# GpSimd's constants at the head of its program, two scalings on ScalarE, first tokens in two transfers, other priorities in a macaron transformer layer

## The chip, the cores and the metric

The kernel runs on one core of one Trainium2 chip, in one launch. The metric is the device time of that core in microseconds (us); lower is better. The core's engines are TensorE (PE in the rows; its weight loads are PEld), VectorE (DVE), ScalarE (ACT), GpSimd (POOL) and the queue that issues the transfers, SyncE (SP).

## The reference, cut to what matters

Eight batches of 512 tokens of width 256 in float32 pass through a feed-forward block with an attention over the 16 heads of each single token and 8 experts, through an attention over the 512 tokens of a batch with 8 heads, and through the first block again with the same weights.

```python
x = hidden_states                                     # (8, 512, 256)
x = x + 0.5 * ffn(layernorm(x))
x = x + attn(layernorm(x))                            # 8 heads of 32, softmax over 512 keys
x = x + 0.5 * ffn(layernorm(x))

def ffn(x):
    h = rmsnorm(x, gamma1)
    q = h @ Wq + bq                                   # 16 heads of 16
    k, v = split((h @ Wdown + bdown) @ Wup + bup)     # 256 -> 64 -> 512
    att = softmax(q k^T / 4) over the 16 heads of the same token
    x = x + (att v) @ Wo + bo
    h2 = rmsnorm(x, gamma2)
    gate = softmax(h2 @ Wg + bg)                      # 8 experts
    return x + sum_e gate[e] * (h2 @ We[e])
```

## The kernel before

All tokens stay in SBUF in `X` (128 partitions, 8 batches, 4 tiles of 128 tokens, 256). Products are made of float32r pairs: an operand is held as a high and a low part (`_hi`, `_lo`) and three products are added. A feed-forward block of one batch is a **job**: jobs 0 to 7 are the first pass, 8 to 15 the second (`k` in the code; B is 8). Each job has these steps, and a step is one entry in an engine's program:

- `stats` (VectorE, L1020 and L1024: mean and variance of four tiles) and `norm` (GpSimd, L1530 to L1542: seven small instructions that make the factors; for job 0 it is cut into `norm_first`, L1504 to L1516, and `norm_outer`).
- `xs` (GpSimd, L1563): the tokens scaled, in two halves p of two tiles each. `hT` (TensorE, L757) transposes a half, `hT_hi` (ScalarE, L1315) and `hT_lo` (VectorE, L1074) take it out of PSUM.
- `down`, `q`, `key`, `val` (TensorE products, L503), `q_turn`, `key_turn`, `val_turn` (VectorE, L1100, L1111, L1124), `key_P`, `key_A`, `val_P`, `val_A` (GpSimd L1571 and ScalarE L1338: the copies that the products per token need), `scores` (TensorE, L673, 64 small products), `top`, `exp`, `at`, `attend` (TensorE, L683), and so on to the `expert` products (L503 with `we`), whose sums are added by VectorE (`add`, L1236) and by ScalarE and GpSimd (`y` L1390, `ysum` L1616 to L1621).
- Between the two passes the attention over tokens runs: `score` (TensorE L906), `max` (VectorE L1262), `shift` (TensorE L916), `a_exp` (ScalarE L1453), `a_total` (VectorE L1268), `normalise` (GpSimd L1665, 64 times), `values` (TensorE L932), `a_add` (GpSimd L1626). For job 8 `xs` also waits for the attention's last transposes out of the same buffer (`a_hT`), and fills the last column of its tokens with ones first (L1560, a memset).

GpSimd's program starts with constants (L1483 to L1493). Four more, the step `blank` (L1518 to L1522: `la_one`, the zero halves of `qc`, `one_v`, `at`), stand in its order after `norm_outer`. TensorE's program starts with 16 transposes of nothing (L712) and has 10 and 16 more ahead of key(0, 1) and scores(0).

The head also prepares weights: `last` and `columns`, `spread`, `fold`, `gate_fold`, `gate_last`, `gate_row` bring gamma and the biases into the weights; `gate_out` (TensorE, 12 products of 8 columns with `late`) and `gate_wo` (VectorE, L1058 to L1060) add the gate's columns to `wo`; `split_hi` (ScalarE L1276) and `split_lo` (VectorE L990) make the two parts; `we_lo` (GpSimd L1552) does it for the experts. `split_lo` 1, the low part of `wq`, must be there before q(0, 0).

What each engine does in which order is not written out. `all_steps` (L78) lists every step with its engine, a duration in ns and the steps it follows; `all_orders` (L298) plays them through: whenever an engine is free, it takes the step of highest rank among those that can start now. The rank is the longest way to the end of the program plus a weight for the kind of step (`SOONER`) and for the batch (`FIRST`); TensorE adds `SAME` for a step that uses the array the same way as the one before it (`ARRAY`: `score` in row tiles, `values`, `scores`, `attend` in column tiles). Durations and landing times in that list are the author's entries; the chip only runs the resulting orders, with semaphores between them. The order inside the attention over tokens is written out by hand (`ATTENTION`, L43), but which other step comes in between is chosen by rank. `stats` of jobs after 8 can only come after the attention's last `max`.

The transfers are issued by SP one after the other (L1681 on): the first batch's tokens in one transfer of 512 KB (L1678), then gamma's row, the last rows of two weights, the biases, the weights, the next batches.

Of the kernel before, what the change touches and what calls it, by code (L numbers as in the profile page):

```python
# [9 lines left out]
ACT = mybir.ActivationFunctionType  # L10
# [61 lines left out]

def parts_of(job, B):

    return 2 if job in (0, B) else 1


def all_steps(B, NT, KC):  # L78
# [8 lines left out]
    for s, landed in enumerate((4400, 12000, 16500, 18500)):  # L87
        put("SP", landed, ("tokens", s))
# [3 lines left out]
    for n, (landed, hi, lo) in enumerate(((5600, 300, 300), (7000, 650, 1300), (7700, 650, 0), (9500, 650, 1700),  # L92
                                          (12900, 650, 1300), (7600, 0, 0), (22500, 1900, 1250), (24500, 1900, 1250),
# [14 lines left out]
    put("PE", 640, ("spread", 0), ("last", 0))  # L108
    put("PE", 2560, ("spread", 1), ("last", 0))
# [3 lines left out]
    put("DVE", 250, ("gate_fold", 0), ("load", 5))  # L113
    put("PE", 400, ("gate_last", 0), ("gate_fold", 0))
    put("DVE", 250, ("gate_row", 0), ("gate_last", 0), ("load", 1))
    put("SP", 13300, ("turned", 0))
    put("PE", 1700, ("gate_out", 0), ("gate_fold", 0), ("turned", 0))
    put("DVE", 400, ("gate_wo", 0), ("gate_out", 0), ("load", 4))
    for s in range(2 * B):
# [4 lines left out]
        put("DVE", 1730, ("stats", s), ("x1_base", s - 4, 1), ("wo", s - 2, 1), ("tokens", s), ("max", 2 * units - 1) if s > B else None, *((("a_add", 2 * (s - B) + 1), ("v", B - 1, 1)) if s >= B else ()))  # L124
# [149 lines left out]
def array(step):  # L274
# [3 lines left out]
SOONER = {"h2_hi": 155309, "v_bias": 130160, "x1": 118233, "gate_log": 112513, "key_P": 100350, "v_out": 96048, "rms2": 87786,  # L278
          "v": 80851, "square": 78299, "tokens": 73022, "gate_fold": 71677, "ct": 68435, "a_xs": 68192, "down": 61079,
          "wo": 59315, "attend": 58763, "la_hi": 52648, "part": 51519, "h2_lo": 50672, "split_hi": 48886, "one_v": 43448,  # L280
          "exp": 42343, "a_back": 39349, "inverse": 36900, "oT": 35898, "y": 35590, "q_zero": 33280, "at_zero": 31562,
          "scores": 30424, "score": 27358, "out_turn": 25962, "mult": 24751, "key_A": 24548, "hT": 22341, "q_turn": 21869,
          "q": 21212, "a_hT_lo": 18697, "half": 16917, "gate_out": 15487, "key_turn": 13862, "gate_row": 11987, "fold": 11330,
          "la_one": 8163, "at": 7258, "val": 5987, "val_P": 4350, "blank": 3716, "xs": 3624, "ysum": 2665, "la_v": 2398,
          "gate_wo": -394, "h2T": -400, "x1_base": -901, "val_A": -1384, "hT_lo": -3409, "rows": -3441, "normalise": -3650,
          "max": -4668, "key": -5820, "finish": -6703, "oT_lo": -10377, "a_hT": -10394, "load": -10984, "a_add": -11291,
          "last": -11698, "norm_outer": -12030, "norm": -13117, "split_lo": -14578, "rest_lo": -14687, "a_rstd": -15325,
          "la_lo": -15389, "qk": -18087, "shift": -20647, "values": -20842, "expert": -20892, "norm_first": -24809,
          "add": -26430, "gate_soft": -27431, "hT_hi": -31815, "spread": -34984, "q_up": -40144, "a_hT_hi": -42271,
# [115 lines left out]
def macaron(nc, a, out):  # L405
# [20 lines left out]
    with ctx:  # L426
# [1352 lines left out]
```

## Time and profile before

| what | value |
|---|---|
| time, median of 3 runs | 1004.2 us (1003.93 to 1006.15) |
| the profiled execution's own time | 1001.64 us |
| its span, first to last instruction | 999.6 us |
| mean granted TensorE clock | 0.987 of full |
| TensorE, VectorE, GpSimd, ScalarE busy | 96%, 85%, 79%, 64% |
| transfers | 14.46 MB, mean 14 GB/s |

The span is 2.0 us shorter than the same execution's time, and that execution was 2.6 us faster than the median. Shares of busy time are of the span. A TensorE share is high even where its matmuls wait for each other, since their ends are modelled; idle time that a row gives with a releaser (`<-`) is time in which the engine had nothing to do until that one had finished.

### The profile page before, as it was taken

What the parts mean: (1) busy time and instruction counts of PE and PEld (TensorE: products, weight loads), DVE (VectorE), ACT (ScalarE), POOL (GpSimd) and SP (SyncE); (2) the same over time, 40 slices, a digit from 0 to 9 for tenths busy, and PEclk for the clock granted to TensorE, in tenths of its full rate; (3) what the DMA queues carried; (4) which work ended last, traced back from release to release, by engine and by line L of the source; (5) the groups of instructions that cost most, each with busy time, mean ns of one, the idle gap of its engine ahead of it and who ended that gap; (6) DMA issues with size and microseconds to landing.
All of it is one profiled execution on the core that took longest, in us unless ns stands there. A gap on an engine that the chain in (4) does not pass through costs nothing.

```text
span 999.6 us, 28140 instructions
## 1 busy us (share of the span) xinstructions
PE 958.4 (96%) x11065; PEld 758.2 (76%) x11065; DVE 852.6 (85%) x1387; ACT 637.6 (64%) x1279; POOL 793.6 (79%) x874
## 2 busy tenths in 40 slices
PE   8799999999999989999999999897999999999998
PEld 7678788888887866666666666456788888888886
DVE  6898998999985379999999999997999889869843
ACT  4767557658554467777777876675775575467542
POOL 6979879879865548999899899997768887598554
PEclk7899999999999999999999999999999999999999
DMA  7021000000000000000000000000000000000001
GB/s 225 2 75 44 3 2 2 2 2 2 3 2 0 2 1 3 1 2 2 2 1 3 1 1 3 2 1 2 3 2 22 17 7 24 1 23 24 2 22 42
DMA packets 8255, 14.46 MB, mean 14 GB/s; under 512 B 1977, under 2 KB 5948, under 8 KB 8126
## 3 DMA queue, kind: packets, MB, share of 16 engines
q1 hardware_dynamic: 8126, 12.67, 3.6%
q8 instruction: 89, 1.46, 0.6%
q14 instruction: 40, 0.33, 0.1%
HBM read 8.48 MB, written 4.19 MB: 13 GB/s over the span
## 4 chain that ended last, share of the span: by engine, by line
PE 80%; DVE 9%; issue 4%; POOL 4%; ACT 2%; DMA 0%; DVEq 0%; POOLq 0%; ACTq 0%
PE psum L503 51%; PE psum L906 6%; PE psum L932 6%; PE psum L916 5%; PE psum L683 4%; PE psum L673 3%; DVE late L1268 2%; DVE oT L1262 2%; PE psum L757 1%; POOL late L1665 1%; PE psum L815 1%; PE psum L830 1%; PE psum L867 1%; DVE kvcs L1111 1%; DVE kvcs L1152 0%
## 5 line engine op out<-in xcount | busy, mean ns | idle before, releaser
L503 PE MATMUL psum<-we,h 128*128 128x512 f32 x1536 | 385.2, 399 | 3.2 <-DVE X L1236 2.4
L503 PEld LDWEIGHTS psum<-we,h 128*128 128x128 f32 x1536 | 280.0, 188 | 64.4 <-issue 4.9
L1390 ACT ACTIVATE late<-psum,gate 128x256 f32<-128x256 f32 x252 | 105.0, 469 | 114.3 <-PE psum L503 57.5
L1236 DVE SCALAR_TENSOR_TENSOR X<-psum,gate,X 128x256 f32<-128x256 f32 x260 | 123.9, 478 | 58.0 <-PE psum L503 49.8
L1262 DVE TENSOR_REDUCE oT<-psum 128x128 fp32r<-128x1024 f32 x128 | 154.9, 1218 | 13.0 <-PE psum L906 12.6
L1453 ACT ACTIVATE kvx<-psum 128x1024 f32<-128x1024 f32 x126 | 128.8, 1024 | 54.4 <-PE psum L916 43.1
L1268 DVE TENSOR_REDUCE late<-kvx 128x256 f32<-128x2048 f32 x63 | 143.4, 2276 | 0.6 <-POOL late L1665 0.6
L1665 POOL TENSOR_TENSOR late<-kvx,late 128x2048 f32<-128x2048 f32 x31 | 121.3, 3912 | 26.1 <-ACT late L1460 16.7
L1616 POOL TENSOR_TENSOR late<-late 128x512 f32<-128x512 f32 x63 | 82.5, 1309 | 65.2 <-ACT late L1390 65.2
L1665 POOL TENSOR_TENSOR kvx<-kvx,late 128x2048 f32<-128x2048 f32 x32 | 125.0, 3907 | 1.6 <-ACT late L1460 0.8
L1338 ACT ACTIVATE kvx<-kvcs,mask 128x512 f32<-128x512 f32 x132 | 88.9, 737 | 24.8 <-DVE kvcs L1111 12.9
L1571 POOL TENSOR_SCALAR kvx<-kvcs,mask 128x512 f32<-128x512 f32 x124 | 86.3, 717 | 12.8 <-DVE kvcs L1111 9.3
L916 PE MATMUL psum<-oT,neg_id 128*128 128x512 f32 x256 | 89.1, 429 | 5.9 <-DVE oT L1262 5.6
L916 PEld LDWEIGHTS psum<-oT,neg_id 128*128 128x128 f32 x256 | 40.5, 188 | 25.3 <-DVE oT L1262 11.0
L906 PEld LDWEIGHTS psum<-kvcs 32*128 32x128 f32 x1024 | 36.8, 185 | 25.8 <-issue 22.8
L503 PE MATMUL psum<-wq,hT 128*128 128x264 f32 x384 | 55.2, 296 | 1.1 <-DVE hT L1074 0.8
L906 PEld LDWEIGHTS psum<-late 32*128 32x128 f32 x1024 | 36.7, 185 | 25.0 <-issue 24.8
L1621 POOL TENSOR_TENSOR X<-X,late 128x256 f32<-128x256 f32 x63 | 47.3, 750 | 9.3 <-POOL late L1618 0.4
L503 PE MATMUL psum<-wo,oT 128*128 128x264 f32 x384 | 52.7, 287 | 1.5 <-DVE oT L1178 1.0
L503 PEld LDWEIGHTS psum<-wq,hT 128*128 128x128 f32 x384 | 51.6, 197 | 3.2 <-issue 1.2
L503 PEld LDWEIGHTS psum<-wo,oT 128*128 128x128 f32 x384 | 50.1, 188 | 4.7 <-issue 2.0
L906 PE MATMUL psum<-kvcs 32*128 32x128 f32 x1024 | 49.3, 295 | 3.7 <-ACT kvx L1453 2.3
(183 smaller groups left out, 1935.1 us busy)
## 6 DMA issues: line engine op xcount, KB each, us to landing
X<-in_L_attn_hidden_states SPq DMA_DIRECT2D x8, 512.0 KB, 5.5
out<-X SPq DMA_DIRECT2D x7, 512.0 KB, 2.6
X<-in_L_ffn_We SPq DMA_DIRECT2D x2, 1024.0 KB, 11.2
out<-X SPq DMA_DIRECT2D x1, 384.0 KB, 2.3
late<-in_L_ffn_turned SPq DMA_DIRECT2D x1, 257.0 KB, 4.5
kvx<-in_L_ffn_Wq SPq DMA_DIRECT2D x1, 256.0 KB, 2.8
kvx<-in_L_ffn_Wup SPq DMA_DIRECT2D x2, 128.0 KB, 2.6
kvx<-in_L_ffn_Wo SPq DMA_DIRECT2D x1, 256.0 KB, 4.2
```

The lines of the kernel that those rows point to most:

```text
L503: ins = e.matmul(out_ap, l, r, start=(n == 0), stop=(n == len(terms) - 1))
L906: ins = e.matmul(psum[:, pair(half) + bank, n * HQN:(n + 1) * HQN], qk[b % 2][rows, 1, hg, m * P:(m + 1) * P], qk[b % 2][rows, 0, hg, q0:q ...
L916: ins = e.matmul(psum[:, bank, :].rearrange("p (g n) -> p g n", n=HQN), neg_id[:, :], mr[g // 2 % 2][:, queries(g)].unsqueeze(1).to_broadc ...
L1236: e.scalar_tensor_tensor(out=xi, in0=psum[:, u % 3, w * D:(w + 1) * D], scalar=gate[k % 2][:, i, 2 * n + w:2 * n + w + 1], in1=xi, op0=ALU ...
L1262: e.tensor_reduce(mr[g // 2 % 2][:, queries(g)], heads(g), AX.X, ALU.max).then_inc(a_max, 1)
L1268: e.tensor_reduce(rec[u % 2][:, :], exponentials(u)[:, :, :], AX.X, ALU.add).then_inc(a_total, 1)
L1338: expand(e, k, name[:3], "A", lambda o, src, m_: e.activation(o, src, ACT.Copy, scale=m_))
L1390: e.activation(y[:, n // 2 * 2 + w, :], psum[:, u % 3, w * D:(w + 1) * D], ACT.Copy, scale=gate[k % 2][:, i, 2 * n + w:2 * n + w + 1]).the ...
L1453: e.activation(exponentials(u)[:, queries(g), :], heads(g), ACT.Exp, scale=float(D) ** -0.5).then_inc(a_exp, 1)
L1571: expand(e, k, name[:3], "P", lambda o, src, m_: e.tensor_scalar(o, src, m_, 1.0, ALU.mult, ALU.mult))
L1616: own.step(e.tensor_tensor(y[:, 0:2, :], y[:, 0:2, :], y[:, 2:4, :], ALU.add))
L1665: e.tensor_tensor(prob[u % 2][:, :, :].rearrange("p g n -> p n g"), exponentials(u)[:, :, :], rec[u % 2][:, :].unsqueeze(2).to_broadcast([ ...
```

## The change

Four things. (1) `blank` is given no predecessor and `norm_first` must follow it, so its four constants stand at the head of GpSimd's program. (2) The step xs(0, 1) and both halves of xs(8, .) move from GpSimd to ScalarE, as two `Identity` activations with scale and bias per half; the memset of ones for job 8 becomes a ScalarE copy of two columns. `norm_outer` may follow xs(0, 0). (3) The first batch's tokens come in two transfers of two tiles each, each with a semaphore of its own, and `stats` of job 0 waits for the second before its third tile. (4) `SOONER`, `FIRST` and `SAME` have other values, some durations of the head are other numbers, and `gate_out` follows `gate_row` in place of `gate_fold`.

```diff
+def scaled_by_act(job, p, B):
+    return job == B or (job, p) == (0, 1)
...
-    for s, landed in enumerate((4400, 12000, 16500, 18500)):
+    for s, landed in enumerate((4000, 12000, 16500, 18500)):
...
-    put("PE", 640, ("spread", 0), ("last", 0))
-    put("PE", 2560, ("spread", 1), ("last", 0))
+    put("PE", 750, ("spread", 0), ("last", 0))
+    put("PE", 1400, ("spread", 1), ("last", 0))
...
-    put("SP", 13300, ("turned", 0))
-    put("PE", 1700, ("gate_out", 0), ("gate_fold", 0), ("turned", 0))
+    put("SP", 12300, ("turned", 0))
+    put("PE", 1350, ("gate_out", 0), ("gate_row", 0), ("turned", 0))
...
-        put("POOL", 3100 if s else 1520, norm, ("stats", s), ("q_turn", s - 4, 1))
+        if s == 0:
+            put("POOL", 5200, ("blank", 0))
+        put("POOL", 3100 if s else 1520, norm, ("stats", s), ("q_turn", s - 4, 1), ("blank", 0))
         if not s:
-            put("POOL", 1900, ("norm_outer", 0), norm, ("xs", 0, 1))
-            put("POOL", 3100, ("blank", 0), ("xs", 0, 1))
+            put("POOL", 2100, ("norm_outer", 0), norm, ("xs", 0, 0))
         for p in range(NT // 2):
-            put("POOL", 1110, ("xs", s, p), norm, ("hT", s - 1, p))
+            put(*(("ACT", 1010) if scaled_by_act(s, p, B) else ("POOL", 1110)), ("xs", s, p), norm, ("hT", s - 1, p),
+                ("a_hT", B - 1, KC - 1) if s == B else None)
...
-FIRST = {0: -997, 1: -2432, 2: -391, 3: 8343, 4: -12195, 5: 5132, 6: -6820, 7: 5276}
-SAME = 5125
+FIRST = {0: 3015, 1: -4321, 2: -1753, 3: -1589, 4: 6574, 5: -1106, 6: -1717, 7: 1431}
+SAME = 9767
...
+        def scaled(k, p):
+            if scaled_by_act(k, p, B):
+                return s_xs_act, 1 if k == 0 else p + 2
+            return s_xs, 2 * k + p + (k == 0) - 2 * (k > B)
...
                 elif name == "hT":
                     p = piece[2]
-                    e.wait_ge(s_xs, 2 * k + p + 1)
+                    e.wait_ge(*scaled(k, p))
...
                 elif name == "gate_out":
-                    e.wait_ge(s_gfold, 1)
+                    e.wait_ge(s_grow, 1)
...
                     for i in range(NT):
+                        if (k, i) == (0, NT // 2):
+                            e.wait_ge(l_x0_rest, 16)
                         ins = e.bn_stats(raw[:, i, :], X[:, s, i, :])
...
+                elif name == "xs":
+                    p = piece[2]
+                    if k == B:
+                        e.wait_ge(a_hT, 2 * B)
+                        e.activation(xs[:, 2 * p:2 * p + 2, D - 1], half_neg[:, 0:2], ACT.Copy, scale=-2.0)
+                    else:
+                        e.wait_ge(s_pad, 1)
+                    e.wait_ge(*normed(k, 1))
+                    for i in (2 * p, 2 * p + 1):
+                        ins = e.activation(xs[:, i, 0:D - 1], X[:, s, i, 0:D - 1], ACT.Identity, bias=negm[k % 4][:, 1, i:i + 1],
+                                           scale=rs[k % 4][:, 1, i:i + 1])
+                    ins.then_inc(s_xs_act, 1)
...
                     p = piece[2]
                     if k:
                         e.wait_ge(s_hT, 2 * k - 1 + p)
-                    if k == B:
-                        e.wait_ge(a_hT, 2 * B)
-                        own.step(e.memset(xs[:, 2 * p:2 * p + 2, D - 1:], 1.0))
...
         def sp_program(e):
-            load_x(e, 0)
+            first_x = x_dram[0].rearrange("(p i) d -> p i d", i=NT)
+            e.dma_start(X[:, 0, 0:NT // 2, :], first_x[:, 0:NT // 2, :]).then_inc(l_x[0], 16)
+            e.dma_start(X[:, 0, NT // 2:, :], first_x[:, NT // 2:, :]).then_inc(l_x0_rest, 16)
```

Of the 98 weights in `SOONER`, all of which have other values, these are spoken of below (before, after): `normalise` -3650, -253970; `stats` -94206, -204214; `norm` -13117, -34746; `split_lo` -14578, 75632; `q` 21212, -103; `gate_out` 15487, -77453.

## Rows read from the trace of the kernel before

**Rows 1.** The page, part 1: busy us, share of the span and instructions.
```profile
PE 958.4 (96%) x11065; PEld 758.2 (76%) x11065; DVE 852.6 (85%) x1387; ACT 637.6 (64%) x1279; POOL 793.6 (79%) x874
```
**Rows 2.** Windows: us; busy us per engine; granted PE clock, DMA share, GB/s.
```profile
27.00:30.00 3.00, 1.64 (x70) 1.31 (x68) 2.32 (x4) 3.00 (x4) 2.85 (x6) 1.00 0.00 0
30.00:33.00 3.00, 0.29 (x12) 0.32 (x16) 1.54 (x3) 3.00 (x6) 3.00 (x6) 0.91 0.01 3
33.00:36.00 3.00, 3.00 (x71) 2.82 (x63) 1.12 (x3) 1.04 (x3) 3.00 (x6) 0.52 0.02 5
...
40.00:60.00 20.00, 17.25 (x272) 14.80 (x270) 18.99 (x34) 11.52 (x27) 14.54 (x21) 0.91 0.17 54
60.00:100.00 40.00, 39.02 (x450) 33.17 (x451) 35.71 (x77) 29.53 (x70) 37.44 (x56) 1.00 0.14 48
```
**Rows 3.** Timeline of TensorE around 30 us: start us, us, engine, line, operation.
```profile
27.54 1.10 PE L673 MATMUL psum<-kvx,qc 128*32 128x64 f32 x64
32.71 2.04 PE L683 MATMUL psum<-kvx,kvcs 128*32 128x68 f32 x64 [4.07 <-DVE kvcs L1152]
```
**Rows 4.** Timeline, 12 to 35 us: `blank`'s first and last memset (of 5), job 1.
```profile
12.79 0.52 POOL L1518 MEMSET la_one<- 66x512 f32 x1
13.26 0.38 DVE L1024 BATCH_NORM_AGGREGATE mv<-bn_raw 128x2 f32<-128x6 f32 x4
14.66 0.95 POOL L1522 MEMSET kvcs<- 128x1024 f32 x1
...
26.22 0.19 POOL L1530 TENSOR_SCALAR rs<-mv 128x4 f32<-128x4 f32 x1
...
29.11 0.20 POOL L1542 TENSOR_TENSOR rs<-rs 128x4 f32<-128x4 f32 x1
...
32.32 2.25 POOL L1563 TENSOR_SCALAR xs<-X,rs,negm 128x255 f32<-128x255 f32 x4
```
**Rows 5.** Timeline: job 0's four scalings on GpSimd, four activations of the same form.
```profile
8.25 2.23 POOL L1563 TENSOR_SCALAR xs<-X,rs,negm 128x255 f32<-128x255 f32 x4
14.04 2.06 ACT L1410 ACTIVATE late<-X,negm,rs 128x256 f32<-128x256 f32 x4
```
**Rows 6.** Timeline of the head: first transfer, last constants, first statistics, `wd`'s low part.
```profile
0.73 0.38 SPq L1678 DMA_DIRECT2D X<-in_L_attn_hidden_states  x1
...
1.95 0.10 POOL L1493 MEMSET xs<- 128x4 f32 x1
...
2.42 0.48 DVE L1003 COPY perm<-ident 128x32 f32<-128x32 f32 x4
...
4.26 1.41 DVE L1020 BATCH_NORM_STATS2 bn_raw<-X 128x6 f32<-128x256 f32 x4 [1.36 <-DMA X<-in_L_attn_hidden_states]
...
7.47 0.29 DVE L990 TENSOR_TENSOR wd<-kvx,wd 128x128 fp32r<-128x128 f32 x1 [0.17 <-ACT wd L1276]
```
**Rows 7.** DMA issues, 0 to 40 us: KB each, us from issue to landing.
```profile
kvx<-in_L_ffn_Wq SPq DMA_DIRECT2D x1, 256.0 KB, 2.8
```
**Rows 8.** Timeline of TensorE, `q` at half clock (24 products) and at full (12).
```profile
16.96 5.55 PE L503 MATMUL psum<-wq,hT 128*128 128x264 f32 x24 [0.30 <-DVE wq L990]
...
37.74 1.71 PE L503 MATMUL psum<-wq,hT 128*128 128x264 f32 x12
```
**Rows 9.** Windows, TensorE's clock in the head (columns as in rows 2).
```profile
18.00:21.00 3.00, 3.00 (x15) 3.00 (x15) 2.25 (x6) 1.13 (x1) 3.00 (x3) 0.50 1.10 354
```
**Rows 10.** Windows, the passage into the second pass (columns as in rows 2).
```profile
600.00:700.00 100.00, 86.07 (x1201) 60.02 (x1194) 90.47 (x98) 65.85 (x109) 91.21 (x67) 0.98 0.01 2
...
640.00:650.00 10.00, 8.08 (x102) 4.61 (x106) 10.00 (x7) 6.69 (x11) 10.00 (x7) 1.00 0.01 2
```
**Rows 11.** Timeline of GpSimd, 649 to 683 us: job 8's first scaling, the last `normalise`, job 9's `norm`.
```profile
649.88 1.15 POOL L1563 TENSOR_SCALAR xs<-X,rs,negm 128x255 f32<-128x255 f32 x2
...
678.37 3.84 POOL L1665 TENSOR_TENSOR kvx<-kvx,late 128x2048 f32<-128x2048 f32 x1
682.30 0.20 POOL L1530 TENSOR_SCALAR rs<-mv 128x4 f32<-128x4 f32 x1
```

More of the change, by code:

```diff
@@ L123, in all_steps @@
         before = parts_of(s - 1, B) - 1
-        put("DVE", 1730, ("stats", s), ("x1_base", s - 4, 1), ("wo", s - 2, 1), ("tokens", s), ("max", 2 * units - 1) if s > B else None, *((("a_add", 2 * (s - B) + 1), ("v", B - 1, 1)) if s >= B else ()))
+        put("DVE", 1730 if s else 1400, ("stats", s), ("x1_base", s - 4, 1), ("wo", s - 2, 1), ("tokens", s), ("max", 2 * units - 1) if s > B else None, *((("a_add", 2 * (s - B) + 1), ("v", B - 1, 1)) if s >= B else ()))
         norm = ("norm", s) if s else ("norm_first", 0)
-        put("POOL", 3100 if s else 1520, norm, ("stats", s), ("q_turn", s - 4, 1))
+        if s == 0:
+            put("POOL", 5200, ("blank", 0))
+        put("POOL", 3100 if s else 1520, norm, ("stats", s), ("q_turn", s - 4, 1), ("blank", 0))
         if not s:
-            put("POOL", 1900, ("norm_outer", 0), norm, ("xs", 0, 1))
-            put("POOL", 3100, ("blank", 0), ("xs", 0, 1))
+            put("POOL", 2100, ("norm_outer", 0), norm, ("xs", 0, 0))
         for p in range(NT // 2):
-            put("POOL", 1110, ("xs", s, p), norm, ("hT", s - 1, p))
+            put(*(("ACT", 1010) if scaled_by_act(s, p, B) else ("POOL", 1110)), ("xs", s, p), norm, ("hT", s - 1, p),
+                ("a_hT", B - 1, KC - 1) if s == B else None)
         for p in range(NT // 2):
@@ L276, in array @@
     return ARRAY.get(step[0], "whole")
[L278 to L289, printed above, removed]
-          "gate_exp": -42772, "gate_sub": -43277, "top": -45983, "mask": -52629, "turned": -53367, "xs2": -54759,
-          "a_total": -55891, "oT_hi": -56347, "x1_norm": -57707, "gate_last": -67776, "columns": -72604, "we_lo": -74579,
-          "a_stats": -76189, "val_turn": -92386, "stats": -94206, "a_exp": -110245}
@@ L294 @@
-FIRST = {0: -997, 1: -2432, 2: -391, 3: 8343, 4: -12195, 5: 5132, 6: -6820, 7: 5276}
-SAME = 5125
+SOONER = {"a_hT_hi": 239643, "x1": 235093, "key_P": 182498, "la_one": 176836, "la_v": 155784, "oT_hi": 140932, "max": 138368,
+          "h2T": 137611, "exp": 135296, "gate_log": 117886, "at": 117467, "gate_row": 114694, "half": 114414, "values": 97202,
+          "v_bias": 92781, "oT": 87935, "square": 76965, "split_lo": 75632, "y": 71685, "a_hT_lo": 70754, "a_total": 55940,
+          "mult": 55314, "tokens": 53178, "one_v": 51667, "norm_outer": 51357, "norm_first": 48657, "a_back": 48394,
+          "h2_hi": 47568, "rms2": 45312, "val": 43794, "la_hi": 42942, "a_exp": 41093, "wo": 40497, "q_turn": 36993,
+          "add": 36487, "key_A": 33892, "out_turn": 28688, "blank": 28214, "q_zero": 24175, "attend": 23122, "a_xs": 20673,
+          "key_turn": 20244, "hT_hi": 20139, "load": 17896, "scores": 8878, "ysum": 8833, "v_out": 8265, "shift": 4957,
+          "xs": 4687, "val_P": 4475, "we_lo": 3725, "hT": 3104, "q": -103, "inverse": -164, "spread": -331, "key": -1982,
+          "down": -2692, "expert": -3003, "ct": -4707, "q_up": -7504, "gate_wo": -13718, "h2_lo": -14792, "rows": -15769,
+          "gate_fold": -17393, "split_hi": -23831, "oT_lo": -24341, "gate_last": -31565, "gate_soft": -34283, "norm": -34746,
+          "at_zero": -36536, "mask": -37671, "part": -44286, "gate_exp": -45447, "columns": -50504, "a_hT": -54764,
+          "val_A": -60744, "a_stats": -62679, "a_rstd": -68230, "xs2": -68582, "x1_base": -77317, "gate_out": -77453,
+          "x1_norm": -84982, "hT_lo": -91111, "gate_sub": -92141, "qk": -93132, "v": -95928, "finish": -99274,
+          "a_add": -115804, "last": -117340, "fold": -117873, "la_lo": -144547, "val_turn": -144670, "turned": -145408,
+          "top": -172455, "score": -178675, "rest_lo": -185126, "stats": -204214, "normalise": -253970}
@@ L463, in macaron @@
         l_x = [sem(f"l_x{b}") for b in range(B)]
+        l_x0_rest, s_xs_act = sem("l_x0_rest"), sem("s_xs_act")
         l_wd, l_rows, l_wq, l_end, l_bias, l_wu = (sem("l_" + n) for n in ("wd", "rows", "wq", "end", "bias", "wu"))
@@ L1525, in pool_program @@
                     if k >= 4:
-                        e.wait_ge(s_xs, 2 * (k - 3))
+                        e.wait_ge(*scaled(k - 4, 1))
                         e.wait_ge(s_x1p, 2 * (k - 3))
```

8 lines of the change are left out of this document (4 added, 4 removed).

## The prediction, made before the changed kernel was run

> **What bounds the kernel now.** The page's first part comes first: TensorE is busy 96% of the span, VectorE 85%, GpSimd 79% [rows 1]. Such an average doesn't say where a microsecond counts, so the windows are read next. From 60 to 100 us TensorE is busy 39.0 of 40 us [rows 2]; there, and in most of both feed-forward passes, only the number and the order of its products matter, and a delay or gain that arrives from before is passed on unchanged. The 41.2 us in which TensorE is idle (999.6 less 958.4) lie elsewhere: 13.9 of them between 600 and 700 us, in the passage from the attention to the second pass [rows 10], and 2.75 between 40 and 60 us with 4.07 in one piece before it, from 28.6 to 32.7 us [rows 2, 3]. Those two places are where this change edits.
>
> In the head TensorE waits at 28.6 us for the first token products. From 27 to 36 us GpSimd is busy 8.85 of 9 us, while VectorE has done only 4.98 [rows 2]: it lacks input. What GpSimd does there is late work: `norm` of job 1 starts at 26.22 and ends at 29.31, `xs` of job 1 ends at 34.57, though the statistics of job 1 were there at 13.64 [rows 4]. At 13.64 GpSimd was filling constants (`blank`, five memsets, 12.79 to 15.61) [rows 4]. TensorE has nothing of job 1 to do in its gap because job 1 isn't scaled. In the passage between 640 and 650 us GpSimd and VectorE are both busy 10.0 of 10 us and ScalarE 6.7 [rows 10].
>
> **The constants at the head.** GpSimd's own constants end at 2.05 us and its first piece of work for data waits for statistics whose first operation alone runs until 5.67 [rows 6], so 2.8 us of memsets (12.79 to 15.61) [rows 4] fit before it: they would end near 4.9. Their cover is the first transfer; without it they would cost up to those 2.8 us. Together with xs(0, 1), half of 2.23 us [rows 5], 3.9 us leave GpSimd's program between 9 and 16 us. After `norm_outer`, which ended at 12.79 and would end one half sooner, near 11.7, GpSimd is free when job 1's statistics arrive at 13.6, and `norm` (3.09 us) and both `xs` halves (2.25 us) [rows 4] can run 10 us earlier. That is worth something only through TensorE's gap. From above: the gap of 4.07 us [rows 3] and, since the clock after it was granted at 0.52 for 3 us [rows 2], another 1.4 us, 5.5 us in all. VectorE sets a tighter limit, for from 40 to 60 us it is busy 18.99 of 20 us [rows 2] and has to do its share of job 1 somewhere: the time it can give is what it idles between 27 and 36 us, 9.0 less 4.98, or 4.0 us. From below: nothing. I take 3.0 us, a microsecond under VectorE's limit, since the wait for the first `attend` itself is not removed and some of its idle time will stay.
>
> **The scalings on ScalarE.** Four activations of this form take 2.06 us where GpSimd takes 2.23 [rows 5], so a half costs ScalarE 1.03 us. For job 0 the two engines would work side by side. The second half that comes earlier I count at nothing by itself, since behind it stands the first half's chain on the same engines; only GpSimd's relief counts, and it is in the term above. For job 8 GpSimd gets rid of two halves of 1.15 us [rows 11], 2.3 us, and of two small memsets; ScalarE gets 2.1 us and two copies of two columns. The work queued behind them on ScalarE is the attention's exponentials, and it has a third of its time free there. From above the gain is 2.3 us, all of it on the critical chain. From below it is a loss of one half, 1.0 us, if the activation stands in front of an exponential that VectorE waits for. As VectorE is as full as GpSimd in that stretch [rows 10], I take 1.0 us.
>
> **The first tokens in two transfers.** A transfer of 256 KB lands 2.8 us after its issue [rows 7], the whole one of 512 KB issued at 0.73 was awaited until 4.26 [rows 6], 3.5 us. The first half then lands near 3.5 and its two tiles are done 0.7 us later. The second half is issued 0.38 us later, and lands between 3.9 (1.11 plus 2.8) and 4.6 (4.24 plus the added issue): the four tiles end between 4.6 and 5.3 instead of 5.67, so 0.3 to 1.0 us sooner. Every transfer behind it on SP's queue is issued about 0.4 us later: gamma's row, the weights, job 1's tokens. `last`, the fold of `wd` and the split follow that row. The low part of `wd` was done at 7.76 [rows 6], and the first `down` has to wait for the first scaled half, ready at 9.4 [rows 5], and its transpose: 1.6 us of cover at least, and with the cover gone it would be the 0.4. I take 0.4 us, as TensorE's work from 12 us on is near dense and would take only part of it; the ends are a loss of 0.4 (if the added issue is what counts) and a gain of 1.0.
>
> One row speaks of a clash: VectorE's last four constants run from 2.42 to 2.90 us with GpSimd idle beside them [rows 6]; after the change GpSimd's memsets run there. No row shows whether they hold each other up. That is a rival below.
>
> **The new weights.** They change no instruction, only orders, on every engine, over the whole span. Here the trace of before shows no price. From above: a third of TensorE's idle time in the passage, some 4.6 of 13.9 us [rows 10], and 2.1 us in the head if the clock is back before the second half of `q` (24 products took 5.55 us at half clock, two times 12 would take 3.42 at full) [rows 8, 9]. `split_lo` now ranks high, and `q` far above `gate_out`, so that q(0, 0) can start right behind the first `down` instead of at 16.96; the products are the same and near dense either way, so I count nothing for it alone. From below: a job's step started too late, about 5 us (the slower rival). Both signs are as near, and I take zero.
>
> **Sum.** 3.0 + 1.0 + 0.4 = 4.4 us less. The profiled execution would go from 1001.64 us to 997.2 (span 999.6 to 995.2). It was 2.6 us faster than the median of its kernel; against the median, 1004.2 less 4.4 is 999.8 us.
>
> **The rivals.** A measurement of this kernel can tell about 0.2% from no change, 2 us.
>
> *More from the order.* The clock is back before q's second half, 2.1 us, and the passage gives another 2: 995.7 us. For it: `SAME` is nearly doubled, so TensorE changes less between whole and tiled use of its array, and the head has a long stretch at half clock [rows 9]. Against it: from 60 us on the products of the feed-forward passes are dense already. Chance 0.16.
>
> *The place stays empty.* `stats` has lost 110,000 in rank and `norm` 22,000. Between 12 and 18 us VectorE has other work of job 0 ready (second `hT_lo`, two `la_lo`, `gate_wo`, the splits), and whatever can start now and ranks higher goes first. If job 1's statistics slide behind it, to 18 us and more, GpSimd idles where `blank` was, `norm` of job 1 stays near its 26.22 [rows 4], and the gap of 4.07 us [rows 3] too. The change then doesn't do what its first part is good for; 0.4 and some tenths remain: 1003.3 us. Chance 0.20.
>
> *Slower: `normalise` starved in the passage.* Its weight falls by 250,000, that of `norm` by 22,000. Before, the last `normalise` ran at 678.37 and `norm` of job 9 after it, at 682.30 [rows 11]. With the new ranks any step of the second pass that can start on GpSimd goes ahead of it. The last `normalise` holds back the last `values` and the finish of the attention, and with them the expansion and `out_turn` of jobs 8 and 9. Price: one `norm`, 3.1 us, and one job's `xs`, 2.2 us [rows 4], 5.3 us. It decides from the point at which GpSimd has no idle time between the arrival of job 9's statistics and the last `normalise`, which the full windows make possible [rows 10]. With the head's 3.4 us kept and nothing won in the passage: 1004.2 less 3.4 plus 5.3, or 1006.1 us. Chance 0.16.
>
> *VectorE's constants held up.* If each copy of VectorE waits for the memset beside it, its constants end with GpSimd's near 4.9 us instead of 2.90, and the first tile's statistics, now possible at 3.5, start at 4.9, 0.6 us later than the 4.26 of before [rows 6]. The 0.4 us turns into a loss of 0.6: 1000.8 us. The Trainium skill says it in "SBUF — State Buffer", section "SBUF: two separate sides": VectorE in a two-port mode and GpSimd lock a shared port pair against each other for a whole instruction. No row of before shows it for memsets. Chance 0.05.
>
> **How the numbers follow.** The forecast has 0.38, the four rivals 0.57; 0.05 is for orders that I can't name, more of it on the slow side. Faster by over 0.2% (under 1002.2) are the forecast, the first and the last rival, nearly all of them: 0.59. Within 0.2% is the empty place and the forecast's weak end: 0.21. Slower by over 0.2% (above 1006.2) takes the starved `normalise` when its price is full and the unnamed orders; as that rival lies on the edge I give it all: 0.20. The forecast's own range is 997.5 to 1002.0. Over all cases, with the weights' unknown on both sides, the range is 995.0 to 1006.3.
>
> **What would show each step.** The constants are right if GpSimd's memsets run between 2 and 5 us, `norm_first` starts no later than before, `norm` of job 1 runs near 14 us and TensorE's gap after the first `scores` is gone or under 2 us, with VectorE busier between 27 and 36. They are wrong if `norm` of job 1 is still past 20 us. The scaling is right if GpSimd's full stretch in the passage ends about 2 us sooner in relation to the first `score`, with ScalarE's activations beside it. The two transfers are right if the statistics start near 3.5 and end before 5.4. The last `normalise` should have no `norm` of job 9 between it and its `inverse`; if it has, the slower rival holds. TensorE's idle time per stage (head, middle, 600 to 700 us, tail) gives the weights' share: anything beyond 4 us there would make the prediction wrong, and so would a head that is 3 us sooner at 60 us with an end that is not.

## The result, and the profile after

The changed kernel takes 996.77 us (median of 5 runs, 995.33 to 998.04), the kernel before 1004.2 (5 runs beside it, 1000.56 to 1006.15). The ratio is 0.9938, with a 95% interval of 0.992 to 0.9956: the medians differ by 7.4 us, and the ratio gives 6.2 (4.4 to 8.0). 999.8 had been forecast, with a range of 995.0 to 1006.3. Profiled execution against profiled execution it is only 3.6 us (1001.64 to 998.04, spans 999.6 and 996.1): the one of before lay 2.6 us under its median, the one of after 1.3 above. Of all the executions told of below one, of parts_old_order, took 1315.82 us at a mean granted clock of 0.651, and its ratio leaves it out.

The page after, part 1, answers to [rows 1]. The instructions are as many, save for GpSimd's 8 fewer and ScalarE's 8 more:

```profile
PE 956.9 (96%) x11065; PEld 757.0 (76%) x11065; DVE 857.5 (86%) x1387; ACT 640.0 (64%) x1287; POOL 787.9 (79%) x866
```

Windows of after, in the columns of [rows 2], whose stretches and those of [rows 10] they answer to:

```profile
27.00:30.00 3.00, 1.72 (x74) 1.42 (x76) 2.33 (x4) 3.00 (x2) 2.84 (x7) 1.00 0.00 0
30.00:33.00 3.00, 1.60 (x101) 1.47 (x105) 2.19 (x4) 2.95 (x6) 3.00 (x6) 1.00 0.03 8
33.00:36.00 3.00, 1.65 (x51) 1.34 (x40) 2.90 (x6) 1.43 (x3) 3.00 (x6) 1.00 0.00 0
...
600.00:700.00 100.00, 87.52 (x1206) 61.01 (x1205) 91.47 (x104) 70.52 (x121) 90.42 (x63) 0.98 0.01 2
640.00:650.00 10.00, 8.48 (x112) 5.18 (x112) 10.00 (x9) 7.49 (x12) 9.26 (x5) 1.00 0.00 0
```

From 27 to 36 us GpSimd is as full as before, and VectorE does 7.42 us of work where it did 4.98: the first hole is smaller. From 600 to 700 us TensorE is busy 87.52 us instead of 86.07. The timeline of after, GpSimd's moved memsets (first and last of five) and VectorE in the head, answers to [rows 6]:

```profile
1.98 0.52 POOL L1546 MEMSET la_one<- 66x512 f32 x1
...
2.27 2.58 DVE L1013 TENSOR_SCALAR neg_id<-ident 128x128 fp32r<-128x128 f32 x1
2.42 2.73 DVE L1017 COPY perm<-ident 128x32 f32<-128x32 f32 x4
...
3.82 0.94 POOL L1550 MEMSET kvcs<- 128x1024 f32 x1
...
5.08 1.39 DVE L1036 BATCH_NORM_STATS2 bn_raw<-X 128x6 f32<-128x256 f32 x4
```

The constants do fit ahead of the data, but VectorE's copies beside them take 2.73 us instead of 0.48, and the first statistics start at 5.08, not at the 3.5 that two transfers should give, nor at the 4.26 of before. Next the timeline of after between 6 and 33 us: `spread`'s products, job 0's second half scaled on ScalarE, the first `down`, `q` of job 0 with `gate_out` between its halves, and job 1, as in [rows 3 to 5, 8]:

```profile
6.00 4.18 PE L511 MATMUL psum<-kvx 1*128 1x64 f32 x12
...
9.03 1.09 ACT L1330 ACTIVATE xs<-X,negm,rs 128x255 f32<-128x255 f32 x2 [0.60 <-POOL negm L1544]
...
13.27 1.22 PE L511 MATMUL psum<-hT,wd 128*128 128x256 f32 x4 [0.76 <-DVE wd L1004]
14.29 2.75 PE L511 MATMUL psum<-wq,hT 128*128 128x264 f32 x12
...
17.35 1.40 PE L511 MATMUL psum<-neg_g,late 128*128 128x8 f32 x12
...
21.54 1.72 PE L511 MATMUL psum<-wq,hT 128*128 128x264 f32 x12 [0.63 <-DVE qc L1116]
...
24.47 1.34 DVE L1036 BATCH_NORM_STATS2 bn_raw<-X 128x6 f32<-128x256 f32 x4
...
26.31 0.19 POOL L1558 TENSOR_SCALAR rs<-mv 128x4 f32<-128x4 f32 x1 [0.22 <-DVE mv L1040]
27.57 1.10 PE L687 MATMUL psum<-kvx,qc 128*32 128x64 f32 x64
29.95 1.10 PE L687 MATMUL psum<-kvx,qc 128*32 128x64 f32 x64 [1.28 <-issue]
32.45 1.16 PE L697 MATMUL psum<-kvx,kvcs 128*32 128x68 f32 x64 [1.40 <-DVE kvcs L1168]
```

Job 1's statistics went from 11.83 to 24.47 us, so its `norm` still starts at 26.31 (26.22 before) [rows 4]. The first `scores` and the first `attend` start where they did (27.54 and 32.71) [rows 3]; what fills part of the hole is the second group of `scores`, at 29.95. (In another execution of the same order all of these start 3 us later; see job 1's section below.) In the passage, ScalarE's and GpSimd's timelines of after answer to [rows 11]:

```profile
631.63 1.08 ACT L1330 ACTIVATE xs<-X,negm,rs 128x255 f32<-128x255 f32 x2
...
676.61 3.77 POOL L1690 TENSOR_TENSOR kvx<-kvx,late 128x2048 f32<-128x2048 f32 x1
680.90 0.19 POOL L1558 TENSOR_SCALAR rs<-mv 128x4 f32<-128x4 f32 x1
```

Job 8's first scaling runs 18 us earlier than at 649.88, and the last `normalise` still runs ahead of job 9's `norm`.

**By stage.** One cut serves for every kernel: the first `score` of the attention (before 355.1 us, after 352.6) and the start of the last `normalise` (678.4 and 676.6). Windows of before, then of after, from the first `score` to the last `normalise`, and from there to the end:

```profile
355.10:678.40 323.30, 309.82 (x3886) 209.81 (x3889) 308.67 (x242) 243.09 (x380) 289.14 (x119) 1.00 0.01 2
678.40:999.60 321.20, 308.23 (x3503) 260.25 (x3493) 256.88 (x518) 184.38 (x429) 231.57 (x337) 0.99 0.04 15
```
```profile
352.60:676.60 324.00, 311.21 (x3902) 210.93 (x3901) 309.23 (x234) 247.13 (x391) 285.31 (x108) 1.00 0.01 2
676.60:996.10 319.50, 307.63 (x3483) 259.50 (x3476) 256.29 (x520) 183.09 (x427) 231.21 (x339) 0.99 0.04 15
```

So the two profiled executions differ by 2.5 us up to the first `score`, by 0.7 the other way in the attention, and by 1.7 after it. How much of that one pair of profiles can tell is said under *The kernel before, once more*.

### The profile page after: what moved, and what is told of

It is laid out like the page before. It is cut to its first block, busy times and chain, and to the rows that moved or that the text cites. A ratio compares the mean times of both kernels' runs of the same rounds, so it can differ in the third digit from the quotient of the medians.

```text
span 996.1 us, 28140 instructions
## 1 busy us (share of the span) xinstructions
PE 956.9 (96%) x11065; PEld 757.0 (76%) x11065; DVE 857.5 (86%) x1387; ACT 640.0 (64%) x1287; POOL 787.9 (79%) x866
## 4 chain that ended last, share of the span: by engine, by line
PE 82%; DVE 9%; POOL 4%; issue 4%; ACT 1%; DVEq 0%; POOLq 0%; ACTq 0%
PE psum L511 53%; PE psum L920 6%; PE psum L930 6%; PE psum L946 5%; PE psum L697 3%; PE psum L687 3%; DVE late L1284 3%; DVE oT L1278 2%; PE psum L829 1%; PE psum L771 1%; PE psum L844 1%; PE psum L881 1%; POOL kvx L1690 1%; DVE qc L1116 1%; DVE kvcs L1168 0%
```

## The experiments

Medians are of 5 rounds (5 to 12 executions) unless said otherwise, ratios against the kernel before on the same chip. The last three columns are the stages just named, from the profiled execution (us); "old" and "new" are the written-out orders of before and after.

| kernel | median | ratio [95%] | stages |
|---|---|---|---|
| before | 1004.2 | 1 | 355.1, 323.3, 321.2 |
| before_again | 1004.28 (one execution) | | 357.8, 323.4, 321.0 |
| after | 996.77 | 0.9938 [0.992, 0.9956] | 352.6, 324.0, 319.5 |
| parts_old_order | 1004.52 | 1.0004 [0.9993, 1.0015] | 356.1, 323.7, 321.1 |
| new_then_old | 1001.72 | 0.9981 [0.9971, 0.999] | 355.1, 324.6, 321.5 |
| old_then_new | 1000.65 | 0.9958 [0.9941, 0.9975] | 356.0, 323.1, 315.6 |
| old_weights | 1019.07 (3 rounds) | 1.0152 [1.013, 1.0175] | 363.8, 326.4, 326.8 |
| xs8_on_gpsimd | 1000.36 | 0.9969 [0.9954, 0.9985] | 351.6, 328.4, 318.5 |
| job1_early | 998.37 | 0.9944 [0.9923, 0.9964] | 355.4, 324.0, 317.6 |
| blank_late | 996.56 | 0.9923 [0.9906, 0.994] | 351.0, 323.9, 319.0 |
| copies_later | 996.44 | 0.9928 [0.9912, 0.9943] | 353.2, 324.0, 318.1 |
| blank_late_one_transfer | 996.66 (3 rounds) | 0.9936 [0.9915, 0.9956] | 351.7, 324.0, 318.8 |
| no_turns | 995.32 | 0.9911 [0.9896, 0.9926] | 352.9, 324.0, 316.6 |
| blank_late_no_turns | 995.59 | 0.992 [0.9902, 0.9938] | 350.5, 324.0, 317.9 |

### The three parts without the new order

The old weights and step list make the lists; then the three parts are put into them by hand.

```diff
+orders["POOL"]: ("blank", 0) first; ("xs", 0, 1), ("xs", 8, 0), ("xs", 8, 1) taken out
+orders["ACT"]: these three put in at the times at which GpSimd had them
 two transfers of the first tokens, and gate_out waiting for gate_row, as in the change
```

> The three edits (constants first, xs(0, 1) and xs(8, .) on ScalarE, first tokens in two transfers) inside the order of steps of the kernel before, nothing else reordered. Theory A (the parts carry the gain, the order is only fitted to them): at least 4 of the 7.4 us between the medians, so a ratio to before of 0.996 or less. Theory B (the reordering carries it): the parts by themselves give little, since the order of before cannot use the GpSimd time that they free, and VectorE's set-up copies are held up beside the moved memsets as in the changed kernel; ratio 0.998 to 1.001, first score near 355 us.

1004.52 us, a ratio of 1.0004: nothing. GpSimd's timeline shows why the freed time isn't used (`blank`'s old place, then job 1's `norm`):

```profile
14.65 0.40 POOL L1673 TENSOR_SCALAR la_one<-la 64x256 fp32r<-64x256 f32 x1 [2.07 <-ACT la L1361]
18.06 0.62 POOL L1673 TENSOR_SCALAR la_one<-la 64x256 fp32r<-64x256 f32 x1 [3.01 <-ACT la L1361]
...
26.79 0.19 POOL L1561 TENSOR_SCALAR rs<-mv 128x4 f32<-128x4 f32 x1
```

GpSimd idles 2.07 and 3.01 us, with job 1's statistics done near 14.5 us (they start at 12.66), but in a written order `norm` stays behind work that isn't ready. By themselves the parts give 0.0 ± 1.1 us, where 4.4 had been counted for them. Each of the three alone wasn't run in this order.

### Where the order works

Each engine's list is cut at the 33rd attention unit, and one side is taken from each order.

```diff
+cut = position of ("values"/"a_total"/"inverse"/"normalise", 32) in each list
+new_then_old: new[:cut] + old[cut:]
+old_then_new: old[:cut] + new[cut:]
```

> All parts of the change. Every engine follows the changed kernel's order up to the 33rd unit of the attention (of 64) and the order of before (with the parts moved, as in parts_old_order) from there on. The two orders hold the same steps on each side of that cut. Theory A (the gain is made in the head and the first pass): about 998.5 us, nearly the whole distance from 1004.5 (parts_old_order) to 996.8. Theory B (it is made in the passage and the second pass): about 1003. Traces so far split the 4.8 us between the spans as 3.5 up to the first score and 1.3 behind it, so my expectation is 1000 to 1001.

> The counterpart: the order of before (with the parts moved) up to the 33rd unit of the attention, the changed kernel's order from there on. Theory A: 1003 us or more. Theory B: about 998. From the traces so far 1002 to 1003. If the halves are independent, the two differences from parts_old_order's 1004.5 add up to 7.7 us.

The new order up to the cut gives 1.0004 − 0.9981 = 0.0023, or 2.3 us (with the intervals of both ratios 0.9 to 3.8); from the cut on, 0.0046, or 4.6 us (2.6 to 6.6). The sum, 6.9 us, agrees with the 6.6 us between parts_old_order and after (0.0066): as far as these intervals tell, the effects add and together are the whole result. Single profiles had led me to expect the larger part in the first half. The windows around the start of the second pass, of before, after and old_then_new in turn:

```profile
680.00:690.00 10.00, 5.63 (x161) 4.56 (x160) 6.82 (x11) 5.93 (x10) 9.60 (x16) 0.95 0.01 2
```
```profile
680.00:690.00 10.00, 7.83 (x169) 6.94 (x170) 5.46 (x9) 4.33 (x7) 9.59 (x19) 0.83 0.01 3
```
```profile
680.00:690.00 10.00, 5.71 (x165) 4.66 (x164) 5.68 (x9) 4.19 (x8) 9.59 (x15) 1.00 0.01 3
679.10:994.70 315.60, 305.80 (x3484) 257.69 (x3476) 255.99 (x521) 183.22 (x427) 231.19 (x339) 1.00 0.04 15
```

In after's execution the clock in this stretch was granted at 0.83, and the same work (161 to 169 products) kept TensorE busy 7.83 us; with 1.00, in old_then_new, 5.71. So some 2 of the 3.9 us by which old_then_new's last stage is shorter than after's (315.6 against 319.5) are the clock of one execution; from the cut on the two kernels have the same order, so the rest isn't the order's either.

### The new weights with the old ones put back

```diff
-SOONER, FIRST, SAME of the change
+SOONER, FIRST, SAME of before
```

> The changed kernel with SOONER, FIRST and SAME of before; the orders are computed anew from the changed list of steps. Theory A (the new weights are better in themselves): between parts_old_order's 1004.5 and 996.8. Theory B (a set of weights fits one list of steps, and any other set is a draw): well over 1004.5, 1010 us or more, with TensorE idle longer in the passage and the first pass.

1019.07 us, 15 us slower than before. The step list has changed (`blank` needs nothing now, three `xs` are on ScalarE, durations differ), and the old weights, which go with the old list, don't suit it. The opposite, the new weights on the old list, wasn't run, nor were weights looked for again for the old list. So it isn't shown whether the good order needs the three parts or could have been had without them. The first `score` comes at 363.8 us, and job 1's `norm` at 31.13.

### Job 8's scalings back on GpSimd

```diff
 def scaled_by_act(job, p, B):
-    return job == B or (job, p) == (0, 1)
+    return (job, p) == (0, 1)
```

In the lists, ("xs", 8, p) moves from ScalarE's to GpSimd's at its planned time; all other orders stay.

> The changed kernel with both halves of xs(8, .) back on GpSimd, with the memset of ones, at the place in its order that corresponds to their place on ScalarE; all else kept. Theory A (GpSimd sets the pace of the passage, as the prediction has it): 1.0 us more than 996.8, at most 2.6. Theory B (VectorE sets it): within 0.5 us. The measure that is finer than the times is the stretch from the first score to the end of the span.

1000.36 us, 3.6 us more than after (by the ratios 3.1, with their intervals 0.7 to 5.5). In the profile it is lost in the attention: 328.4 us against 324.0, and against 323.1 to 324.6 in every other kernel but old_weights. GpSimd's timeline has the first scaling, a late `normalise` and the last one; the window behind it answers to after's 640 to 650:

```profile
630.01 1.14 POOL L1596 TENSOR_SCALAR xs<-X,rs,negm 128x255 f32<-128x255 f32 x2
...
653.96 3.87 POOL L1698 TENSOR_TENSOR late<-kvx,late 128x2048 f32<-128x2048 f32 x1 [2.91 <-PE psum L951]
...
680.01 3.76 POOL L1698 TENSOR_TENSOR kvx<-kvx,late 128x2048 f32<-128x2048 f32 x1
```
```profile
640.00:650.00 10.00, 9.58 (x96) 5.76 (x92) 7.80 (x6) 5.16 (x8) 9.33 (x4) 0.69 0.00 0
```

Two halves of 1.13 us and two memsets stand ahead of the next `normalise`. Later GpSimd waits 2.91 us for products (1.30 us in after at the same step), and the last `normalise` starts 3.4 us later than after's 676.61, though this attention had begun 1.0 us sooner: 4.4 us in all, where the instructions moved are worth 2.3.

Not all of the rest need come from GpSimd. From 640 to 650 us the clock was granted at 0.69 in this execution (1.00 in after's), so TensorE's products took longer there (16 of `score` 1.24 us at 643.99, 0.73 in after), and VectorE, full in after, was busy only 7.80 of 10 us. Seven of this kernel's twelve executions had a mean granted clock of 0.983 to 0.991, of after's five one; the five at 0.993 or more have a median of 998.66 us, 1.9 over after's. No run separates whether GpSimd's delay brought the lower clock or chance did. So in this order, where the scaling stands at 630 us, having it on ScalarE is worth some 1.9 to 3.6 us. In the old order, where it stood at 651.96 and 660.14, the three parts together were worth nothing.

### Constants behind the first normalisation, or the copies behind the memsets

```diff
+orders["POOL"].remove(("blank", 0)); put it behind ("norm_outer", 0)
```

> The changed kernel with the four constants put back behind norm_outer in GpSimd's order, every other order kept. Theory A (the place matters): job 0's la_one or x1_base on GpSimd come later and the time rises by 1 to 3 us against the changed kernel's 996.8. Theory B (GpSimd was idle where the constants stood, 12.5 to 15.1 us in the changed kernel): VectorE's copies neg_id and perm end before 3 us again instead of at 5.15, the first statistics start near 3.6 to 4.3 instead of 5.08, the head is up to 0.8 us sooner until the first scores, and the total is within 1 us of 996.8.

```diff
 VectorE's program
-    neg_id and perm with the other constants
+    neg_id and perm ahead of ("fold", 1)
```

> The changed kernel with VectorE's copies neg_id and perm (L1013, L1017) moved behind gate_fold, so that they no longer stand beside GpSimd's memsets. If the memsets held the copies up (2.58 and 2.73 us in place of 0.23 and 0.48), the copies are short again and the first statistics start 0.8 to 1.5 us sooner, at 3.6 to 4.3. Theory A (a gain in the head is passed on): 996.0 us or less. Theory B (the first scores wait for something else, they start at 27.6 us in both kernels): the first scores stay within 0.3 us of 27.6 and the total within 0.5 us of 996.8.

(In the kernel that ran they stand there, which is at 8.30 us.) Both take VectorE's copies away from GpSimd's memsets. The timelines of VectorE, first blank_late, then copies_later:

```profile
2.27 0.23 DVE L1015 TENSOR_SCALAR neg_id<-ident 128x128 fp32r<-128x128 f32 x1
2.42 0.47 DVE L1019 COPY perm<-ident 128x32 f32<-128x32 f32 x4
3.71 1.40 DVE L1038 BATCH_NORM_STATS2 bn_raw<-X 128x6 f32<-128x256 f32 x4 [0.82 <-DMA X<-in_L_attn_hidden_states]
```
```profile
3.64 1.41 DVE L1040 BATCH_NORM_STATS2 bn_raw<-X 128x6 f32<-128x256 f32 x4 [1.40 <-DMA X<-in_L_attn_hidden_states]
...
8.44 0.69 DVE L1018 COPY perm<-ident 128x32 f32<-128x32 f32 x4
```

The copies are short again (0.47 and 0.69 us), and the statistics start 1.4 us sooner than after's 5.08. The end doesn't move: 996.56 and 996.44 against 996.77, intervals that cover each other. The memsets at the head are worth nothing by themselves, and the collision that they bring costs nothing that five runs can tell.

### One transfer instead of two

```diff
-load_x in two transfers, wait on l_x0_rest
+load_x(e, 0)
```

This is made on top of blank_late, where nothing holds VectorE up.

> blank_late with the first batch's tokens in one transfer again. In blank_late VectorE is free and the first statistics start at 3.71 and end at 5.11. Theory A (the split brings tokens sooner, as predicted 0.3 to 1.0 us): here they start at 4.2 to 4.3 and end near 5.7, and all rows behind gamma's transfer come 0.4 us sooner. Theory B (the added issue takes it back): the aggregation ends within 0.2 us of blank_late's. The total cannot tell, 996.6 plus or minus 1.

```profile
4.33 1.41 DVE L1036 BATCH_NORM_STATS2 bn_raw<-X 128x6 f32<-128x256 f32 x4 [1.45 <-DMA X<-in_L_attn_hidden_states]
5.77 0.38 DVE L1040 BATCH_NORM_AGGREGATE mv<-bn_raw 128x2 f32<-128x6 f32 x4
```

The statistics start at 4.33 instead of 3.71 and end at 5.74 instead of 5.11: two transfers bring them 0.6 us sooner. Those 0.6 us are still there at the first `scores` (25.96 with two transfers, 26.51 with one), at the first `attend` (30.84 and 31.40) and, 0.7, at the first `score` (351.0 and 351.7), with about the same clock in both heads. In the total it stays unresolved (0.9936 against 0.9923).

### Job 1 put where the prediction had it

```diff
+DVE: ("stats", 1) ahead of ("hT_lo", 0, 1)
+POOL: ("norm", 1) ahead of ("la_one", 0, 1), ("x1_base", 0, .) ahead of ("q_zero", 0, 1), ("xs", 1, 0) and ("xs", 1, 1) ahead of ("key_P", 0) and ("key_P", 1)
+PE: ("hT", 1, 0) ahead of ("scores", 1), ("hT", 1, 1) ahead of ("attend", 0)
```

> The changed kernel with job 1 taken up in the place that the constants left: stats(1) ahead of the second hT_lo on VectorE, norm(1) ahead of the second la_one on GpSimd (near 16 us instead of 26.3), xs(1, .) ahead of key_P, the two transposes of job 1 ahead of scores(1) and of attend(0), x1_base of job 0 later. Theory A (the prediction's premise: TensorE's gap before attend(0) is there for want of scaled tokens of job 1): the transpose of job 1 runs near 28 us and the total falls by 2 us or more below 996.8. Theory B (the gap is the chain scores(0), top, exp, at, attend(0), and what job 1 needs behind it waits for the same engines): nothing gained, 0 to 1.5 us more, since key_P and the second key are pushed back by norm(1).

GpSimd's and TensorE's timelines, and behind them TensorE's of new_then_old:

```profile
15.34 0.19 POOL L1638 TENSOR_SCALAR rs<-mv 128x4 f32<-128x4 f32 x1
...
30.74 1.10 PE L767 MATMUL psum<-kvx,qc 128*32 128x64 f32 x64
31.77 0.66 PE L851 MATMUL psum<-ident,xs 128*128 128x128 f32 x4
...
35.62 1.16 PE L777 MATMUL psum<-kvx,kvcs 128*32 128x68 f32 x64 [1.57 <-DVE kvcs L1248]
```
```profile
17.47 2.56 PE L718 MATMUL psum<-neg_g,late 128*128 128x8 f32 x12
...
30.66 1.10 PE L918 MATMUL psum<-kvx,qc 128*32 128x64 f32 x64
...
35.54 1.16 PE L928 MATMUL psum<-kvx,kvcs 128*32 128x68 f32 x64 [1.39 <-DVE kvcs L1399]
```

This is the picture that I had forecast: `norm` of job 1 at 15.34 us, TensorE's gap filled with job 1's transposes. It takes 998.37 us, 0.6 us (by the ratios) to 1.6 (by the medians) more than after; nothing is gained. The first `scores` and the first `attend` start 3.2 us later than after's 27.57 and 32.45, but that isn't job 1's doing. In new_then_old, where every engine has after's instructions in after's order up to the cut, they are as late. In both of these executions the clock was still at its lower level when `gate_out` ran (2.56 us; 1.40 in after's, from 17.35).

Held against new_then_old, at about the same clock, job 1's work puts off the first `scores` and the first `attend` by 0.1 us each, and job 1's two transposes run 5 us sooner (31.77 and 33.39 instead of 36.62 and 38.69). Yet the first `score` of the attention comes at 355.4 for new_then_old's 355.1. So filling the gap costs the chain next to nothing, doesn't shorten it, and the work done early is worth nothing later. What takes it up further on stays open.

### The transposes of nothing ahead of the first scores

Ahead of `scores` of step 0 after has 16 transposes whose result isn't used (1.91 us, from 25.73). They are left out.

```diff
-turn_nothing(e, 16)
```

> The changed kernel without the 16 transposes of nothing ahead of scores(0) (25.73 to 27.57 us in its trace). They stand in front of scores(0) although key_P ended at 24.0 and q_zero at 24.4. Theory A (the head's end is set by the chain through scores(0)): scores(0) starts 1.8 us sooner and, since ScalarE splits the expert weights from 26.44 to 30.14 us ahead of exp(0), attend(0) moves by less than that; total 0.5 to 1.5 us less than 996.8. Theory B (the clock pays for it): TensorE is idle longer and its products after 30 us run at half clock, total equal or up to 2 us more.

TensorE's timeline, the first `scores` and the first `attend`:

```profile
26.14 1.10 PE L687 MATMUL psum<-kvx,qc 128*32 128x64 f32 x64
...
32.61 2.04 PE L697 MATMUL psum<-kvx,kvcs 128*32 128x68 f32 x64 [1.17 <-DVE kvcs L1165]
```

The first `scores` come 1.4 us sooner, the `attend` doesn't, and runs at half clock (2.04 us instead of 1.16). Up to the first `score` its profile shows nothing won (352.9 for 352.6). The profiled gain is in the last stage (316.6 against 319.5), where the edit changes nothing and old_then_new, with the same order there, has 315.6. With 995.32 us (994.59 to 995.62) and 0.9911 it is the fastest of the kernels here and beats before for certain; its interval touches after's. Both edits together:

> The changed kernel with the constants back behind norm_outer and without the 16 transposes of nothing ahead of scores(0): the two edits that did not lose by themselves (ratios 0.9923 and 0.9911 to before, 0.9938 for the change). If they add up: 0.990 to 0.991, about 994.5 us, scores(0) near 25 us or earlier. If the first gained only by the clock of its profiled execution: 0.991, as without it.

995.59 us: they don't add up.

### The kernel before, once more

> The kernel before, unchanged, for a second profile. The profiled execution of before took 1001.64 us, 2.6 below its median, and that of the changed kernel 998.04, 1.3 above. If that is chance between executions, this profile has another span, 1001 to 1003 us, with the surplus in TensorE products at half clock in the head. If a profile always runs faster than the others, it is 999.6 again.

1004.28 us in one execution, span 1002.2, against 999.6 in the first profile. The first `score` comes at 357.8 instead of 355.1, the later stages last 323.4 and 321.0. Identical code differs by 2.7 us in the first stage alone, as much as before and after differ there in one pair of profiles. New_then_old and after, which are the same program up to the cut, differ there by 2.5 us (355.1 and 352.6). So a stage isn't compared through a pair of profiles, but through the ratios of the two hybrids. All the profiles together do bear these out: the last stage lasted 321.0 to 321.5 us in the four with the old order there and 315.6 to 319.5 in the nine with the new one (old_weights, with an order of its own, left out).

## Why the prediction was right or wrong

**Direction and range** were right, the size wasn't: 7.4 us between the medians for a forecast of 4.4 (by the ratio 6.2, 4.4 to 8.0), and 996.8 lies outside the forecast's own range (997.5 to 1002.0). That the sum came so near is luck: the parts that its terms price give 0.0 ± 1.1 us in the old order, and the 6.6 us came with the term put at zero. Nearest to what happened is the first rival, *more from the order* (995.7 us, chance 0.16), but it had the order add 4.1 us to parts that already gave 4.4.

**The constants at the head, 3.0 us: failed.** The memsets ended at 4.76, near the 4.9 worked out. The step that failed is "GpSimd is free when job 1's statistics arrive at 13.6, and `norm` can run 10 us earlier": they aren't done until 26.2, since the new weights put them behind job 0's work, as the rival *the place stays empty* had it. That rival's place was right, its price (1003.3) not, as the order paid elsewhere; it also leaves out the 1.0 us of the scalings, which would have stayed (1002.8). And the premise below it fell too: job1_early fills place and gap and is no faster. TensorE's idle time in the gap was read as a lack of work. It is the chain from the first `scores` to the first `attend` on VectorE and ScalarE, and work put into the gap neither shortens it nor, by 0.1 us, lengthens it.

**The scalings on ScalarE, 1.0 us: mis-sized**, some 1.9 to 3.6 in the new order; in the old one all three parts together gave 0. The bound of 2.3 from above took the moved instructions alone, and not the waits behind them (2.91 us in place of 1.30), of which the clock of that execution has a share that isn't separated.

**Two transfers, 0.4 us:** the statistics would have started at 3.7 (3.5 was worked out) and ended at 5.1 (4.6 to 5.3), 0.6 us sooner. In the changed kernel that is covered by the copies. The cover of 1.6 us that was counted for the low part of `wd`, done at 7.76 before, is gone: in after the first `down` waits 0.76 us for it, until 13.27. No run prices that alone.

**The new weights, 0: failed**, by 6.6 us, 2.3 up to the 33rd attention unit and 4.6 after. Both signs were "as near" only by the trace of before, which can't price an order. The clock that the rival counted on is a matter of the execution: `q` of job 0 is now split, and took 2.75 and 1.72 us in after's, 4.47 in all instead of 5.55 [rows 8], but 2.84 and 2.49 in new_then_old's, with the same order. Which weights give the 6.6 us isn't settled.

***`normalise` starved*: didn't happen.** The last `normalise` starts at 676.61, ahead of job 9's `norm`, as before [rows 11]: a low rank costs nothing where nothing ready ranks higher. ***VectorE's constants held up*** (chance 0.05) did: VectorE's copies took 2.58 and 2.73 us and ended at 5.15, near GpSimd's 4.76, and the statistics started at 5.08 for the 4.9 worked out. The Trainium skill's rule in "SBUF — State Buffer", section "SBUF: two separate sides", that VectorE in a two-port mode and GpSimd lock each other out of a shared port pair, agrees with this trace in that VectorE was held up, here by memsets; the profile doesn't show VectorE's mode. The rule speaks of one instruction. Here VectorE was held up through the whole run of memsets: `neg_id` (0.23 us without them) began at 2.27, while the first one ran, and ended at 4.85, after the last. Its price in the total isn't the 1.0 us that separates that rival from the forecast; blank_late and copies_later, without the collision, are faster by less than their intervals can tell.

## What to carry to other kernels

Before an idle gap is given a price, ask whether the engine lacks work or waits for a chain that filler doesn't shorten; only an experiment that fills it tells. Before two profiles are compared, look at the time of one group of products of known shape in both: a different clock moved the first `scores` by 3 us in one and the same program. In a kernel with written-out orders a part moved to another engine is worth what the order makes of it (three parts gave nothing in the old order, one of them some 1.9 to 3.6 us in the new), so price part and order together, and search the weights again after each change of the step list. And profile the old kernel twice before reading a difference of 2 us between stages.

## What the hardware showed that was not expected

**The clock's record can miss a stretch at half speed.** Windows of after and of blank_late, the same 3 us each:

```profile
12.00:15.00 3.00, 2.24 (x11) 1.84 (x10) 2.65 (x5) 2.95 (x7) 0.47 (x3) 1.00 0.57 137
```
```profile
12.00:15.00 3.00, 3.00 (x15) 3.00 (x15) 2.87 (x6) 2.98 (x7) 3.00 (x6) 0.50 0.48 103
```

After's column says 1.00 and blank_late's 0.50, yet the same 12 products of `q` take 2.75 us in the one and 2.74 in the other, and 1.72 us later in both. In the head of after's profile the durations have to be believed, not the column.

**One program meets the clock at different times.** `spread`'s 12 products took 4.18 us from 6.00 in after (and in copies_later, no_turns and old_then_new). In new_then_old, which has after's program up to the cut, TensorE's timeline has:

```profile
5.65 2.21 PE L718 MATMUL psum<-kvx 1*128 1x64 f32 x12
```

So in after's execution the lower level, 1.2 GHz, is there with these products at the latest and is over by `gate_out` at 17.35 (12 products in 1.40 us). In new_then_old's it comes behind them, 2 us later or more, and `gate_out` at 17.47 still runs in it (2.56 us). The first `scores` start at 27.57 in the one and at 30.66 in the other. That is 3.1 us between executions of the same instructions, more than the 2.3 us that the new order gives up to the 33rd attention unit. What decides it stays open.
